# Later-stage work re-placed step by step in the last two chunks of a first attention, with its norm and biases applied by ScalarE

## The reference, cut to what matters

```
x = x + attention1(layernorm(x))      # 16 heads of 64; k gets a position table added; W_out, b_out
s = layernorm(x)                      # the input of the second layer
a = s + attention2(s)                 # 16 heads of 8; Wq,bq Wk,bk Wv,bv Wo,bo
a = layernorm(a)*ln1_g + ln1_b
e = mod(floor(a @ router_w + router_b), 4)
f = relu(a @ W1[e] + b1[e]) @ W2[e] + b2[e]
return x + layernorm(a + f)*ln2_g + ln2_b
```

## Time and profile before

| | |
|---|---|
| runs | 2523.77, 2522.16, 2515.28 us (median 2522.16) |
| profiled execution | 2518.01 us, its span 2516.1 us |
| busy | PE 2287.2 us (91%), DVE 1808.1 (72%), POOL 1220.3 (48%), ACT 1134.6 (45%) |
| mean granted clock of TensorE | 0.949 of full |
| chunk 30, chunk 31 | start 1366.88 and 1413.70 us (first exponential after step 0's first scores) |
| end of the first attention | 1481.65 us (copy of its last output starts) |
| first scores of the second attention | 1535.80 us |

### The profile page before, as it was taken

How to read it: one execution, slowest core, us unless ns; L and a number is a source line. 1 busy time by engine, 2 the same in 40 slices (tenths; PEclk the granted TensorE clock), 3 DMA queues, 4 the chain that set the end, 5 groups by cost and what they waited for, 6 DMA issues and landing times. The chain is left out here.

```text
span 2516.1 us, 35332 instructions
## 1 busy us (share of the span) xinstructions
PE 2287.2 (91%) x13030; PEld 1088.1 (43%) x13030; DVE 1808.1 (72%) x2916; ACT 1134.6 (45%) x1215; POOL 1220.3 (48%) x711
## 2 busy tenths in 40 slices
PE   5999999999999999999999978888899889988985
PEld 3455555555555555555555433222233323332333
DVE  6777777777778777777777666888777767776712
ACT  0334444444444444444444312666555545555561
POOL 1676867776867768677766722310300130022012
PEclk8999999999999999999999865999899979997997
DMA  3000000000000000000000000000000000000000
GB/s 106 1 1 1 1 1 1 1 1 1 1 1 1 1 1 1 1 1 1 1 1 18 1 0 1 1 1 1 1 1 1 1 5 1 1 1 5 1 5 5
DMA packets 12261, 11.26 MB, mean 4 GB/s; under 512 B 2112, under 2 KB 10944, under 8 KB 11968
## 3 DMA queue, kind: packets, MB, share of 16 engines
q1 hardware_dynamic: 12096, 9.01, 1.2%
HBM read 7.69 MB, written 1.05 MB: 3 GB/s over the span
## 5 line engine op out<-in xcount | busy, mean ns | idle before, releaser
L850 POOL TENSOR_TENSOR accp<-accp,prob 128x1024 f32<-128x1024 f32 x316 | 777.9, 2462 | 97.4 <-ACT prob L747 66.5
L747 ACT ACTIVATE prob<-scores 128x1024 f32<-128x1024 f32 x512 | 524.9, 1026 | 641.5 <-PE scores L452 611.7
L1136 DVE TENSOR_REDUCE mxp<-ring 128x1 f32<-128x512 f32 x1024 | 636.7, 680 | 201.6 <-PE ring L427 201.5
L1264 DVE TENSOR_REDUCE mxp<-ring 128x1 f32<-128x512 f32 x1024 | 634.8, 682 | 142.6 <-PE ring L543 136.0
L759 ACT ACTIVATE prob<-scores 128x1024 f32<-128x1024 f32 x512 | 495.4, 1022 | 301.0 <-PE scores L561 301.0
L464 PE MATMUL acc_o<-prob,v 128*64 128x512 f32 x2048 | 505.9, 615 | 0.0
L543 PE MATMUL ring<-k_all,q_all 32*128 32x512 f32 x1024 | 386.1, 519 | 128.6 <-DVE mxp L1264 94.9
L447 PE MATMUL scores<-q_all,k_all 64*128 64x512 f32 x3072 | 473.7, 409 | 0.0
L447 PEld LDWEIGHTS scores<-q_all,k_all 64*128 64x128 f32 x3072 | 274.8, 185 | 180.8 <-issue 129.0
L427 PE MATMUL ring<-k_all,q_all 64*128 64x512 f32 x1024 | 283.5, 426 | 36.9 <-DVE mxp L1136 32.1
L888 POOL TENSOR_SCALAR rounded<-kf,parts_sb 128x512 fp32r<-128x512 f32 x31 | 49.5, 1597 | 515.2 <-DVE kf L1251 515.2
(11 more groups left out here) (138 smaller groups left out, 1530.0 us busy)
## 6 DMA issues: line engine op xcount, KB each, us to landing
w_all<-w_pairs SPq DMA_DIRECT2D x1, 1344.0 KB, 10.1
pos_sb<-pos SPq DMA_DIRECT2D x1, 1024.0 KB, 5.7
w_sb<-w SPq DMA_DIRECT2D x4, 256.0 KB, 4.8
mrow<-m_rows SPq DMA_DIRECT2D x64, 2.0 KB
w_all<-w SPq DMA_DIRECT2D x1, 1024.0 KB, 5.6
q_all<-m_rows SPq DMA_DIRECT2D x64, 2.0 KB
out<-ff SPq DMA_DIRECT2D x4, 256.0 KB, 2.3
wout_sb<-wout_pairs SPq DMA_DIRECT2D x1, 512.0 KB, 7.1
```

The lines of the kernel that those rows point to most:

```text
L747: nc.scalar.activation(prob[:, T % SLOTS1, :, :], sc[T % 2][:, :, :], ACT.Exp, scale=SCALE1).then_inc(exp_done, 1)
L850: nc.gpsimd.tensor_tensor(accp[:, k % 2], accp[:, k % 2], prob[:, T % SLOTS1], ALU.add).then_inc(pool_acc, 1)
L1136: done(nc.vector.reduce_max(mxp1[k % 2][:, h * QT + q, kc:kc + 1], bank[:], AX.X), ("max", k, q, kc, h))
L1264: done(nc.vector.reduce_max(mxp2[n % 2][:, h * QT + q, kc:kc + 1], bank[:], AX.X), key)
```

## The change

The work ahead of the second attention is placed anew. ScalarE does the norm (as scale and bias of one activation, for which GpSimd computes one more row), all the `T2` copies, and all biases of `K2` and `Q2` but that of `K2` 0,3, which VectorE now splits straight from its bank. Two of the last chunk's additions go from VectorE to GpSimd, and the four products that normalise the last output go from VectorE to GpSimd too. Chunk 31 has two `max2` tiles in each half step. `V2` 1 and `K2` 1,2 stand behind the first attention, and twelve of the sixteen early tiles of block 1 behind the first two groups of scores of the second attention.

```diff
-LAST_POOL_ADDS = 7
-LAST_DVE_ADDS = 7
+LAST_POOL_ADDS = 9
+LAST_DVE_ADDS = 5
...
-         (CHUNKS1 - 2, 3): [("T2", 0)], (CHUNKS1 - 2, 4): [("K2", 0, 0)], (CHUNKS1 - 2, 5): [("Q2", 0)],
+         (CHUNKS1 - 2, 2): [("T2", 0)], (CHUNKS1 - 2, 3): [("K2", 0, 0)], (CHUNKS1 - 2, 4): [("Q2", 0)],
...
+NORMS1 = {(CHUNKS1 - 2, 1): 0, (CHUNKS1 - 1, 1): 1, (CHUNKS1 - 1, 6): 2}
...
     n = 2 * j + half
-    if n < 8:
-        return tiles[2 * n:2 * n + 2]
-    return tiles[16 + 4 * (n - 11):16 + 4 * (n - 10)] if 11 <= n < 15 else []
+    return tiles[2 * n:2 * n + 2]
...
+    return ([("sums", LAST1), ("V2", 1), ("y", LAST1)] + tiles(2) + [("T2", 3), ("K2", 0, 3), ("K2", 1, 2)] + tiles(3)
+            + [("fin2", 0), ("K2", 1, 3)] + EARLY_TILES[:4])
...
             scores2(0, 0)
             scores2(0, 1)
+            for it in EARLY_TILES[4:]:
+                item2(it)
...
+            def norm2(c):
+                act.wait_ge(rstd_ready, c + 1)
+                for q in range(QT):
+                    t = c * QT + q
+                    last = nc.scalar.activation(s_sb[:, t, :], x1[:, t, :], ACT.Identity, scale=lnv[:, c, 4, q:q + 1],
+                                                bias=lnv[:, c, 5, q:q + 1])
+                last.then_inc(s_ready, 1)
...
+            def plus_bias(key, bias):
+
+                n = order2.index(key)
+                if n == 0:
+                    act.wait_ge(kl_ready, NC * PAIRS)
+                elif order2[n - 1] in SPLIT_BY_DVE:
+                    wait_free(act, order2[n - 1])
+                elif order2[n - 1][0] == "K2":
+                    act.wait_ge(k2_ready[order2[n - 1][1]], order2[n - 1][2] + 1)
+                else:
+                    act.wait_ge(q2_ready, order2[n - 1][1] + 1)
+                wait_full(act, key)
+                nc.scalar.activation(kf[:], ring[bank_of(key)][:], ACT.Identity, bias=bias).then_inc(free[bank_of(key)], 1)
...
+                nc.gpsimd.tensor_tensor(onorm[:, cols], oraw[:, 0, cols], rec[:, cols], ALU.mult).then_inc(onorm_ready, 1)
...
+            def split_keys2(key):
+
+                g, b = key[1:]
+                before = order2[order2.index(key) - 1]
+                dve.wait_ge(k2_ready[before[1]], before[2] + 1)
+                bank, bias = open_(key), bqk_sb[:, g, 1:2]
+                link(nc.vector.tensor_scalar(rounded[:], bank[:], bias, parts_sb[:, 1:2], ALU.add, ALU.mult))
```

More of the change, by code:

```diff
@@ L206, in tiles @@
         return [("max2", 0, h, q, kc) for q in range(QT) for h in (2, 3, 0, 1)]
-    early = [("max2", 1, h, 0, kc) for kc in range(NC) for h in (2, 3, 0, 1)]
-    return ([("sums", LAST1)] + tiles(2)[:6] + [("y", LAST1)] + tiles(2)[6:] + [("T2", 3), ("K2", 0, 3)] + early[:4]
-            + tiles(3) + early[4:8] + [("fin2", 0), ("K2", 1, 3)] + early[8:])
+    return ([("sums", LAST1), ("V2", 1), ("y", LAST1)] + tiles(2) + [("T2", 3), ("K2", 0, 3), ("K2", 1, 2)] + tiles(3)
+            + [("fin2", 0), ("K2", 1, 3)] + EARLY_TILES[:4])
+EARLY_TILES = [("max2", 1, h, 0, kc) for kc in range(NC) for h in (2, 3, 0, 1)]
 def end2():
@@ L776, in item2 @@
                     copy_side(it, v2[:, b * QT:(b + 1) * QT, :, 0:D2], bank[:].rearrange("p (t h n) -> p t h n", t=QT, h=H2))
-                elif it == ("T2", NC - 1):
+                elif kind == "T2":
                     copy_side(it, xnt[:, it[1] * CW:(it[1] + 1) * CW], bank[:])
+                elif kind == "Q2":
+                    plus_bias(it, bqk_sb[:, it[1] % GROUPS, 0:1])
+                elif kind == "K2" and it not in SPLIT_BY_DVE:
+                    plus_bias(it, bqk_sb[:, it[1], 1:2])
                 elif kind == "ot":
@@ L802, in _ @@
                             exps(T)
+                    if (k, j) == (CHUNKS1 - 2, 0):
+                        act.wait_ge(ld2, 16 * LOADS2)
+                        act.wait_ge(ld3, 16 * LOADS3)
+                    if (k, j) in NORMS1:
+                        norm2(NORMS1[k, j])
                     it = last_item1(k, j)
@@ L810, in _ @@
                 copy_o1(k)
-            act.wait_ge(ld3, 16 * LOADS3)
             for it in start2():
+                if it == ("T2", NC - 1):
+                    norm2(NC - 1)
                 item2(it)
@@ L890, in split2 @@
                 nc.gpsimd.tensor_tensor(to, kf[:], rounded[:].bitcast(F32), ALU.subtract).then_inc(ready, 1)
-            order2 = [it for it in USES if it[0] in ("K2", "Q2") and it not in SPLIT_BY_DVE]
+            pool_splits = [it for it in order2 if it not in SPLIT_BY_DVE]
             def split_of(it):
-                n = order2.index(it)
+                n = pool_splits.index(it)
                 if it[0] == "K2":
@@ L973, in _ @@
                         split_keys(*last_item1(k, 3)[1:])
+                    if t == 8 and k == CHUNKS1 - 2:
+                        late(k, 3)
                     if t == 10 and k == CHUNKS1 - 2:
                         late(k, 4)
+                    if t == 5 and k == LAST1:
+                        late(k, 2)
+                    if t == 7 and k == LAST1:
+                        late(k, 3)
+                    if t == 8 and k == LAST1:
+                        deviations(0, 2, stats2, rstd_ready)
                 if last_item1(k, 6) and last_item1(k, 6)[0] == "K":
@@ L978, in _ @@
                 if k == CHUNKS1 - 2:
-                    late(k, 5)
                     late(k, 6)
-            late(LAST1, 4)
-            deviations(0, 2, stats2, rstd_ready)
             late(LAST1, 5)
             late(LAST1, 7)
+            pool.wait_ge(o_copied, CHUNKS1)
+            wait_full(pool, ("y", LAST1 - 1))
+            for q in range(QT):
+                cols = slice(q * 128, (q + 1) * 128)
+                if q < QT - 1:
+                    pool.wait_ge(rec_ready, QT * LAST1 + q + 1)
+                else:
+                    wait_free(pool, ("sums", LAST1))
+                nc.gpsimd.tensor_tensor(onorm[:, cols], oraw[:, 0, cols], rec[:, cols], ALU.mult).then_inc(onorm_ready, 1)
             pool.wait_ge(pv_done, STEPS1 * CHUNKS1)
@@ L1415, in _ @@
                             reciprocals(k - 1, q)
-                    if j == 2 and k >= CHUNKS1 - 2:
-                        norm2(k - CHUNKS1 + 2)
                     it = last_item1(k, j)
@@ L1447, in _ @@
                     mred2(0)
-                elif it == ("max2", 0, 2, 2, 2):
-                    stats_of(3)
-                elif it == ("T2", 3):
-                    norm2(3)
+                item2(it)
+                if it == ("y", LAST1):
+                    stats_of(NC - 1)
+            for it in EARLY_TILES[4:]:
                 item2(it)
```

108 lines of the change are left out of this document (38 added, 70 removed).

## The result

| | before | after |
|---|---|---|
| median, us | 2518.72 (4 runs, 2505.14 to 2523.77) | 2491.78 (4 runs, 2476.95 to 2496.48) |
| ratio of the runs | | 0.9886, 95% interval 0.9849 to 0.9922 |
| profiled execution, its span | 2518.01, 2516.1 | 2494.19, 2492.4 |
| mean granted clock | 0.949 | 0.951 |

The change makes the kernel faster by 1.1%. The forecast was 2485 with a range of 2472 to 2501.

What follows compares the result with a forecast made beforehand. TensorE waits, and its clock falls, from chunk 30 to the second attention's start. Gains 4.2 + 20.7 + 7.6 + 1.0 = 33.5 us off 2518.0 give 2485; range 2472 to 2501.

Steps and rivals of the forecast that it cites:

- The bound: Loss sits from chunk 30 to the second attention's start, where TensorE waits; the rest untouched but for bias sums.
- Chunk 30: Norm, `T2` copy and bias sums leave VectorE; gain 4.2 us, bounds 0 and 5.6.
- The sum is the stop and its clock: In chunk 30, gain is TensorE's 2.67 us stop plus slowed value matmuls (3.48 - 1.94): 4.2 us.
- ScalarE's norm: In chunk 30, four 128x128 operations take ScalarE about 1.1 us, hidden by TensorE's value work.
- Chunk 31: From its first exponential to its last values 47.2 us instead of 67.95, a gain of 20.7.
- four tiles at VectorE's rate, 2.4: At chunk 31's end, four tiles at 0.60 us each take 2.4 us.
- The stretch: From chunk 31's last values to the second attention's third group of scores: 48.7 us instead of 56.3, gain 7.6.
- The second attention: 22 bias sums move from VectorE to ScalarE; gain 1.0 us, between 0 and 3.7.
- GpSimd as bound of chunk 31: In chunk 31, late GpSimd results stop TensorE; price 6 to 12 us, total 2493; chance 0.20.
- The clock: Denser chunk 31 carries 2.4 GHz into the second attention; 9 us more gain, total 2476; chance 0.13.
- ScalarE held in front of its exponentials: In both attentions, bias sums waiting for GpSimd's splits delay exponentials; 42 us against 33, total 2527; chance 0.04.
- Gain given back: Time leaving chunk 31 returns behind it, a third of the gain left; total 2508 to 2515; chance 0.07.

Runs made afterwards that it cites:

- second pair: Changed kernel and kernel before, both unedited, profiled once more: whole times 2477.78 us and 2521.75 us.
- maxima_first: Against the changed kernel, VectorE's two additions of step 0 go behind the four maxima in chunks 30 and 31: 2484.76 us (1 run).
- on_vector: Against the changed kernel, norm, copies of `T2` 0 to 2 and bias sums stay on VectorE: ratio to the kernel before 0.9910.
- first pair: Changed kernel and kernel before as first profiled, unedited: profiled executions of 2494.19 us and 2518.01 us.
- no_defer: Against the changed kernel, the twelve deferred tiles go back ahead of the second attention's first scores: 2500.88 us (1 run).
- pool_load: Against the changed kernel, GpSimd gets four extra buffer fills in chunk 31, behind its split of `K2` 0,1: 2497.76 us (1 run).
- stats_late: Against the changed kernel, the first two blocks' statistics go behind the additions and tiles of step 0 in chunks 30 and 31: 2501.71 us (1 run).

## Why the prediction was right, by its own steps

**The bound.** Right in the main. The three stages the prediction named hold most of the gain, 26 to 30 us of it against 32.5 in the sum, and the first attention up to chunk 30 is within 1 us of before. But block 0 of the second attention, which the prediction put at nothing, gained 4.4 and 7.2 us in the two pairs, with the clock.

**Chunk 30**, gain forecast 4.2, measured 2.7 (2.6 in the second pair). "The sum is the stop and its clock" was true of the old stop. The step that is missing is the statistics: they moved ahead of additions and maxima of step 0, and with the additions they made a stop of 2.03 us, where it had been 0.72. `maxima_first` takes 42.1, within the forecast 42 to 43.

**ScalarE's norm**, forecast 1.1 for four. Too small: it takes 1.64, in chunk 30, while GpSimd adds, and behind the first attention, while GpSimd is idle:

```profile
1378.10 1.64 ACT L784 ACTIVATE pos_sb<-x,lnv 128x128 f32<-128x128 f32 x4
...
1475.02 1.65 ACT L784 ACTIVATE pos_sb<-x,lnv 128x128 f32<-128x128 f32 x4 [8.12 <-POOL lnv L930]
```

That it was hidden was right: no exponential was late behind it. The same norm on VectorE took 3.18 and 3.88 beside GpSimd's additions in `on_vector`, and 1.10 alone. The Trainium skill, "SBUF — State Buffer", section "SBUF: two separate sides", says that ScalarE never waits on anyone there; the trace agrees, with 1.64 beside the additions and 1.65 without.

**Chunk 31**, forecast 47.2, measured 49.8 three times; the gain forecast as 20.7 was 18.1 in the first pair and 14.2 in the second, whose kernel before had more of the clock. From the first exponential to that of step 6 it took 38.1 us (1411.66 to 1449.78) where the terms give 28.9, seven products of 6.9 and 2.8 of waits, 38.6: the steps are a little longer than summed and the wait at the start 0.79 instead of 2.8. What failed is "four tiles at VectorE's rate, 2.4": two additions of 3.43 us stand ahead of them. The end took 11.7 us instead of 8.6, and the stop of 1.26 and the 1.74 that the clock took from the values behind it are 3.0 of the difference. Those two additions met a split by GpSimd and took 3.43 us, where the next two took 2.54; the prediction had warned of that. Clock 0.95 and no "issue" stop, as forecast; the values took 17.2 us in sum, near the 15.5 named.

**The stretch**, forecast 48.7, measured 46.8, just under the 47 to 51 named. The two groups of sixteen tiles end 19.0 and 34.2 us in (forecast 19.8 and 34.4), the maxima are written at 1497.68, 36.2 us in (forecast 35.4). Two terms were too large. From there to the scores at 1501.30 were 3.6 us, not 5.0: TensorE was still at `K2` 1,3 and four tiles, and no wait for the DMAs shows. To the third group it took 7.0, not 8.3, since TensorE fills banks ahead and needs only nine of the twelve maxima before it comes to those scores. The deferral itself is worth 2.1 (`no_defer`).

**The second attention**, forecast 1.0, measured 1.5 in blocks 1 to 3 and 0 in most later ones. It is not what was priced: from 1536 us on TensorE waits 3.7 us, 14 times, for ScalarE's bias sums, as it did for VectorE's.

**The rivals.** GpSimd as bound of chunk 31 is refuted by `pool_load` (2 us of room); one chunk earlier it does bind, as `stats_late` shows. The clock did not stay up: 0.50 in the window from 1501.30, as before. But it came back earlier in block 0, which gave about half or more of that rival's 9 us. ScalarE held in front of its exponentials does not occur in the changed kernel; with the statistics late it occurs once and costs 1.02 us. Gain given back: not by the chain, but for the profiled pair by block 4, 11 us, which another execution did not give back.

**The number.** It is right in part by luck. Terms and measurement differ by 2 to 6.5 us in the three stages (32.5 against 30.4 and 26.0), less than what block 0 gave unpriced, and block 4 took 11 us from the one pair of profiled executions and gave 9 to the other. The rest of the distance from 2485 to 2491.78 lies within what block 4 and its like do. In all the changed kernel ran 14 times, from 2476.95 to 2503.77, and the kernel before beside it 22 times, from 2505.14 to 2531.74. One figure on the way was added up wrong: the highest ends of the terms (5.6, 23.5, 11 and 3.7) and the clock's 9 give 2465, not 2470; nothing else uses it.

**Left open:** why the clock comes back 7 us into block 0 in one execution (55.3 us) and some 20 us into it in two others (60.2 and 60.3), why one stop drops the clock and its twin doesn't, and whether the change alters how often.
